# Four edits to a transformer-layer kernel: how tiles are cut into transfers, how many buffers they have, and where the softmax sums are applied

## The reference, cut to what matters

```python
# x: (2, 8192, 1024) fp32; 16 heads of 64, 4 KV heads; 8 experts, 2 picked, and a shared MLP
xn = layernorm(x)
q, k, v = xn @ Wq, xn @ Wk, xn @ Wv          # rotary embedding on q and k
attn = softmax(q @ k.T / 8 + slope[h] * (j - i))    # ALiBi bias, no causal mask
a = (attn @ v) @ Wo
scores = softmax(xn @ gate_w.T); w_dense = the two largest of 8, others 0
h = xn @ W1[e].T; y, g = split(h)            # H = 768
z = sum_e w_dense[:, e] * ((y * silu(g)) @ W2[e].T) + shared_mlp(xn)
return x + a + z
```

## Time and profile before

| | us |
|---|---|
| two runs | 4456.20 and 4581.11 |
| their median | 4518.65 |
| the profiled execution, whole | 4454.75 |
| its span, slowest core (core 4) | 4453.2 |
| spans of all eight cores | 4438.6 to 4453.2 |

### The profile page before, as it was taken

One profiled execution on the slowest core, in us unless ns is written; L12 is line 12 of the kernel. 1 busy time (PEld: TensorE's weight loads), 2 busy tenths in 40 slices (PEclk: granted clock), 3 DMA queues, 4 the chain that ended last, 5 costly groups with the idle time before them and its releaser, 6 DMA issues. The chain is left out here.

```text
span 4453.2 us, 37344 instructions; the slowest of 8 cores (4438.6 to 4453.2 us)
## 1 busy us (share of the span) xinstructions
PE 3047.1 (68%) x12380; PEld 1144.5 (26%) x12536; DVE 1251.3 (28%) x1819; ACT 1433.3 (32%) x1561; POOL 34.4 (1%) x49
## 2 busy tenths in 40 slices
PE   2333333222778888968888988699999999999611
PEld 1111111111112222221122222244444444444311
DVE  4554554553210000022000000133233333222333
ACT  1111111110557788925578886000110001100000
POOL 0000000000000000000000000000000000000000
PEclk8656656555668999986689999899999999999855
DMA  3111111102000000000000000522102221110133
GB/s 86 50 52 48 50 52 47 38 19 38 0 0 1 1 1 1 1 38 0 1 1 1 1 1 19 104 43 40 32 15 42 43 43 29 24 34 1 36 97 93
DMA packets 112874, 136.21 MB, mean 31 GB/s; under 512 B 10408, under 2 KB 90280, under 8 KB 112688
## 3 DMA queue, kind: packets, MB, share of 16 engines
q0 software_dynamic: 22752, 52.45, 6.7%
q1 hardware_dynamic: 89936, 81.36, 6.2%
HBM read 169.43 MB, written 16.78 MB: 42 GB/s over the span
## 5 line engine op out<-in xcount | busy, mean ns | idle before, releaser
L67 ACT ACTIVATE PT_B<-PS_B,alibi_sb 128x1024 bf16<-128x1024 f32 x626 | 694.1, 1109 | 426.8 <-PE PS_B L67 426.0
L67 PE MATMUL PS_B<-Qpair,K 64*128 64x512 bf16 x1252 | 429.0, 427 | 161.2 <-ACT PT_B L67 146.6
L67 ACT ACTIVATE PT_A<-PS_A,alibi_sb 128x1024 bf16<-128x1024 f32 x428 | 476.6, 1113 | 117.1 <-PE PS_A L67 82.4
L67 PE MATMUL PVB<-PT_B,V 128*65 128x512 bf16 x1252 | 442.1, 440 | 45.1 <-DVE prewo L67 44.5
L67 PE MATMUL PA<-xn,w1sb 128*128 128x512 bf16 x1881 | 438.4, 390 | 33.8 <-DVE wbc L67 28.2
L67 PE MATMUL PB<-xn,w1sb 128*128 128x512 bf16 x1882 | 421.9, 379 | 2.0
L67 PE MATMUL TP<-id_sb,xntm 128*128 128x128 bf16 x640 | 80.9, 306 | 499.6 <-DVE xntm L67 366.1
L67 ACT ACTIVATE gact<-PA 128x1024 f32<-128x1024 f32 x60 | 61.4, 1023 | 871.4 <-PE PA L67 871.4
L67 ACT ACTIVATE lns<-vvs,eps_sb 128x1 f32<-128x1 f32 x80 | 23.5, 294 | 826.4 <-DVE vvs L67 826.4
L67 PE MATMUL PVA<-PT_A,V 128*65 128x512 bf16 x856 | 276.9, 406 | 10.1 <-ACT PT_B L67 10.0
L67 PE MATMUL PS_A<-Qpair,K 64*128 64x512 bf16 x856 | 275.5, 404 | 7.2 <-ACT PT_A L67 6.9
(11 more groups left out here) (121 smaller groups left out, 2375.2 us busy)
## 6 DMA issues: line engine op xcount, KB each, us to landing
xt<-xb SPq DMA_DIRECT2D x256, 128.0 KB, 2.4
w1sb<-w1t POOLq DMA_DIRECT2D x20, 1536.0 KB, 17.0
w2sb<-w2t POOLq DMA_DIRECT2D x20, 768.0 KB, 9.6
xt<-xown SPq DMA_DIRECT2D x64, 128.0 KB, 2.4
zacc<-zst SPq DMA_DIRECT2D x16, 512.0 KB, 2.6
zin<-zacc SPq DMA_DIRECT2D x32, 256.0 KB, 3.5
xtb<-xown SPq DMA_DIRECT2D x64, 128.0 KB, 3.5
out<-osb SPq DMA_DIRECT2D x64, 128.0 KB, 2.0
```

The lines of the kernel that those rows point to most:

```text
L67: ins = getattr(e, m)(*a, **kw)
```

## The change

It makes four edits and leaves the arithmetic as it is.

1. Stage A: `xt` has two slots instead of four, and a tile comes with one transfer of 128 x 1024 instead of four of 128 x 256. SP waits for tile `tau - 2`.
2. Stage B: `pend_evac`, `defer` and the closures are gone. At every pair's end the code records `recB`, `recA`, `nrmB`, `nrmA` in place, before the next pair.
3. Stage C: each of `w1` and `w2` comes with one transfer instead of two.
4. Stage D: `zin`, `xtb` and `out` come and go with one transfer each instead of two, four and four, and all buffers of the stage, `PO` included, have four slots instead of two. The order on SP, with its wait at line 1091, stays.

```diff
-            if tau >= 4:
-                r.wait("sync", V, v_xt_done[tau - 4])
-                r.wait("sync", S, s_xt_done[tau - 4])
-            sxp = sx[tau % 4]
-            for ch in range(4):
-                r.op("sync", "dma_start", xt[:, tbx + ch * 256: tbx + (ch + 1) * 256],
-                     src_r[:, lt, ch * 256:(ch + 1) * 256], inc=[(sxp, 16)])
+            if tau >= 2:
+                r.wait("sync", V, v_xt_done[tau - 2])
+                r.wait("sync", S, s_xt_done[tau - 2])
+            sxp = sx[tau % 2]
+            r.op("sync", "dma_start", xt[:, tb:tb + 1024], src_r[:, lt, :], inc=[(sxp, 16)])
...
-                if it < len(pend_evac):
-                    pend_evac[it]()
...
-            if defer:
-                def chunk1():
-                    recA()
-                    nrmB()
-                pend_evac = [recB, chunk1, nrmA]
-            else:
-                recB(); recA(); nrmB(); nrmA()
-                pend_evac = []
+            r.wait("scalar", T, t_pv[len(kcs) - 1])
+            r.op("scalar", "activation", rtmp[64:65, 0:1024], PVB[64:65, :], AF.Ln)
+            r.chain("scalar")
+            r.op("scalar", "activation", rlb[64:65, 1024:2048], rtmp[64:65, 0:1024],
+                 AF.Exp, scale=-1.0, inc=[(S, 1)])
+            s_recB = S.v
...
+            for head, PVx, hh, s_rec in ((1, PVB, hB, s_recB), (0, PVA, hA, s_recA)):
+                r.wait("tensor", S, s_rec)
+                for st in range(2):
+                    r.op("tensor", "matmul", PVx[64:128, st * 512:(st + 1) * 512],
...
-        for ch in range(2):
-            r.op("gpsimd", "dma_start",
-                 w1sb[:, buf * 12288 + ch * 6144: buf * 12288 + (ch + 1) * 6144]
-                 .rearrange("p (dc f) -> p dc f", dc=4),
-                 w1_d[e].rearrange("(dc p) f -> p dc f", p=128)[:, ch * 4:(ch + 1) * 4, :],
-                 inc=[(gw[buf], 16)])
+        r.op("gpsimd", "dma_start",
+             w1sb[:, buf * 12288:(buf + 1) * 12288].rearrange("p (dc f) -> p dc f", dc=DC),
+             w1_d[e].rearrange("(dc p) f -> p dc f", p=128), inc=[(gw[buf], 16)])
...
-        bb = (tb % 2) * 1024
-        s4p = s4[tb % 2]
-        if tb >= 2:
-            r.wait("sync", V, v_used[tb - 2])
-        for ch in range(2):
-            r.op("sync", "dma_start",
-                 zin[:, bb + ch * 512: bb + (ch + 1) * 512].rearrange(
-                     "p (dc c) -> p dc c", dc=4),
-                 z_r[:, ch * 4:(ch + 1) * 4, tb * 128:(tb + 1) * 128], inc=[(s4p, 16)])
-        for ch in range(4):
-            r.op("sync", "dma_start", xtb[:, bb + ch * 256: bb + (ch + 1) * 256],
-                 xo_r[:, tb, ch * 256:(ch + 1) * 256], inc=[(s4p, 16)])
+        bb = (tb % 4) * 1024
+        s4p = s4[tb % 4]
+        if tb >= 4:
+            r.wait("sync", V, v_used[tb - 4])
+        r.op("sync", "dma_start", zin[:, bb:bb + 1024].rearrange("p (dc c) -> p dc c", dc=DC),
+             z_r[:, :, tb * 128:(tb + 1) * 128], inc=[(s4p, 16)])
+        r.op("sync", "dma_start", xtb[:, bb:bb + 1024], xo_r[:, tb, :], inc=[(s4p, 16)])
...
         r.wait("sync", V, V.v)
-        for ch in range(4):
-            r.op("sync", "dma_start", out_d[tb * 128:(tb + 1) * 128, ch * 256:(ch + 1) * 256],
-                 osb[:, bb + ch * 256: bb + (ch + 1) * 256], inc=[(so[tb % 2], 16)])
-        ds_out[tb] = so[tb % 2].v
+        r.op("sync", "dma_start", out_d[tb * 128:(tb + 1) * 128, :], osb[:, bb:bb + 1024],
+             inc=[(so[tb % 4], 16)])
+        ds_out[tb] = so[tb % 4].v
```

More of the change, by code:

```diff
@@ L178, in build_nc @@
     gset = Ctr(top, nc, "gset")
-    sx = [Ctr(top, nc, f"sx{i}") for i in range(4)]
+    sx = [Ctr(top, nc, "sx0"), Ctr(top, nc, "sx1")]
     scs = Ctr(top, nc, "scs")
@@ L183, in build_nc @@
     ga = [Ctr(top, nc, "ga0"), Ctr(top, nc, "ga1")]
-    s4 = [Ctr(top, nc, "s4a"), Ctr(top, nc, "s4b")]
-    so = [Ctr(top, nc, "so0"), Ctr(top, nc, "so1")]
+    s4 = [Ctr(top, nc, f"s4_{i}") for i in range(4)]
+    so = [Ctr(top, nc, f"so{i}") for i in range(4)]
     sdbg = Ctr(top, nc, "sdbg")
@@ L761, in build_nc @@
                 v_qpair = V.v
[L762 to L801, removed]
-                    else:
-                        v_pvA_free = V.v
-                    v_prewo_done = V.v
-                return emit
@@ new lines, in build_nc @@
+            r.op("scalar", "activation", rtmp[64:65, 0:1024], PVB[64:65, :], AF.Ln)
[3 more added lines that the diff above has]
+            s_recB = S.v
+            r.chain("scalar")
+            r.op("scalar", "activation", rtmp[64:65, 0:1024], PVA[64:65, :], AF.Ln)
+            r.chain("scalar")
+            r.op("scalar", "activation", rlb[64:65, 0:1024], rtmp[64:65, 0:1024],
+                 AF.Exp, scale=-1.0, inc=[(S, 1)])
@@ L824, in build_nc @@
+            s_recA = S.v
             if p < 7 and not do_prebuild:
                 v_qpair, v_psA_next = emit_qbuild(p + 1, gate_s=sB[63], gate_t=t_qkB)
-            t_pv_prev = t_pv_last
+            for head, PVx, hh, s_rec in ((1, PVB, hB, s_recB), (0, PVA, hA, s_recA)):
+                r.wait("tensor", S, s_rec)
+                for st in range(2):
+                    r.op("tensor", "matmul", PVx[64:128, st * 512:(st + 1) * 512],
+                         ones64[64:65, 0:64],
+                         rlb[64:65, head * 1024 + st * 512: head * 1024 + (st + 1) * 512],
+                         start=True, stop=True, skip_group_check=True)
+                r.inc_last("tensor", T)
+                t_bc = T.v
+                r.wait("vector", T, t_bc)
+                ro = (hh % 2) * 64
+                co = (hh // 2) * 1024
+                for st in range(2):
+                    r.op("vector", "tensor_copy", rb_sb[:, :],
+                         PVx[64:128, st * 512:(st + 1) * 512])
+                    r.op("vector", "tensor_mul",
+                         prewo[ro:ro + 64, co + st * 512:co + (st + 1) * 512],
+                         PVx[0:64, st * 512:(st + 1) * 512], rb_sb[:, :],
+                         inc=[(V, 1)])
+                if head == 1:
+                    v_pvB_free = V.v
+                else:
+                    v_pvA_free = V.v
@@ L827, in build_nc @@
+            v_prewo_done = V.v
+            t_pv_prev = t_pv[len(kcs) - 1]
             sA63_prev = sA[63]
@@ L1034, in build_nc @@
     d_sc = ExitStack()
-    zin = d_sc.enter_context(nc.sbuf_tensor("zin", [128, 2048], F32))
-    xtb = d_sc.enter_context(nc.sbuf_tensor("xtb", [128, 2048], F32))
-    zhi = d_sc.enter_context(nc.sbuf_tensor("zhi", [128, 2048], BF16))
-    zhi32 = d_sc.enter_context(nc.sbuf_tensor("zhi32", [128, 2048], F32))
-    zlo = d_sc.enter_context(nc.sbuf_tensor("zlo", [128, 2048], BF16))
-    osb = d_sc.enter_context(nc.sbuf_tensor("osb", [128, 2048], F32))
-    PO1 = d_sc.enter_context(nc.psum_tensor("PO1", [128, 1024], F32))
-    PO2 = d_sc.enter_context(nc.psum_tensor("PO2", [128, 1024], F32))
+    zin = d_sc.enter_context(nc.sbuf_tensor("zin", [128, 4096], F32))
+    xtb = d_sc.enter_context(nc.sbuf_tensor("xtb", [128, 4096], F32))
+    zhi = d_sc.enter_context(nc.sbuf_tensor("zhi", [128, 4096], BF16))
+    zhi32 = d_sc.enter_context(nc.sbuf_tensor("zhi32", [128, 4096], F32))
+    zlo = d_sc.enter_context(nc.sbuf_tensor("zlo", [128, 4096], BF16))
+    osb = d_sc.enter_context(nc.sbuf_tensor("osb", [128, 4096], F32))
+    POs = [d_sc.enter_context(nc.psum_tensor(f"PO{i}", [128, 1024], F32))
+           for i in range(4)]
     r = Rec(SELFS)
```

57 lines of the change are left out of this document (18 added, 39 removed).

## The result

| | before | after |
|---|---|---|
| median of all runs | 4544.62 (26) | 4449.01 (27) |
| fastest run | 4445.55 | 4400.16 |
| profiled execution, whole | 4454.75 | 4404.17 |
| spans of the eight cores | 4438.6 to 4453.2 | 4393.5 to 4402.6 |

The change makes the kernel faster by 1.2%: the ratio is 0.988, with a 95% interval of 0.9846 to 0.9913. The two medians lie further apart than that, because both kernels have executions in which some cores ran at a lower clock; the ratio leaves these out. On 4454.75 us the ratio is 53 us, with the interval 39 to 69. I had forecast 28 less, a ratio of 0.994, which lies outside. So the direction was right and the size was not.

A forecast was written before the change was run, and what follows sets the result against it. Four stages with different limits: A a chain of short steps, B PE and ACT, C PE's speed, D a serial loop. 4454.75 - 26 (D) - 2 (B) + 0 (A, C) gave 4427 us, range 4390 to 4500 for 8 in 10.

The forecast's parts named there:

- Stage D, -26: Stage D: merging ten issues a tile into three saves 1.6 us a tile, 26 us over 16 tiles.
- bounds of 1.0 and 4.2: Stage D, gain in us a tile: 1.0 if the data rate limits, 4.2 if only issues and one large landing count.
- Stage A and C, 0: Stages A and C: no gain or cost, A's transfers staying hidden and C's first weight wait ending with the same byte.
- Stage B, -2: Stage B: ten turns at +0.1 us each and two turns from pair 5 to 6 at -1.5 each, together -2 us.
- The bound of -18: Stage B's largest gain from the rows: ten turns at -0.9 us and two at -4.3.
- Rival 1: Stage D is bound by issue, not data, and gains up to 67 us: 4386 us in all; chance 0.12.
- Rival 2: Stage D: the merged transfers bring nothing, 4453 us in all; chance 0.15.
- Rival 4: Stage A loses its cover from a 9.25 us landing on; at 11 us it costs 140 us, 4567; chance 0.02.
- Rival 3: Stage B: in-place sums cost what the first chunk loses, 6.15 us a turn, 74 us: 4503 in all; chance 0.10.
- Within 2%: Whole kernel: time changes by no more than 2%, between 4366 and 4544 us; chance 0.91.
- Slower: Whole kernel: slower by over 2%, above 4544 us; chance 0.05.
- The likeliest case's own range: Whole kernel: 4405 to 4441 us, with stage D's gain between 16 and 40 and B's between -10 and +4.

The follow-up runs named there:

- d_only: The kernel before with stage D's edit alone (merged transfers, four slots); stage D 233.7 us, ratio 0.9966 [0.9916, 1.0016].
- ac_only: The kernel before with the edits of stages A and C alone; A 1070.8 us, C 1395.5 us, ratio 0.9988 [0.9954, 1.0021].
- before_fill: The kernel before, deferral kept, with throw-away matmuls in PE's wait in a pair's second chunk; stage B 1695.0 us, whole run 4427.77 us.
- b_in_place: The kernel before with stage B's edit alone, sums in place at all 12 turns; stage B 1698.8 us, ratio 0.995 [0.9923, 0.9976].
- fill_chunk: The changed kernel with one throw-away matmul in each B-only chunk after the prebuild; stage B 1679.4 us, ratio 0.9896 [0.979, 1.0003].
- d_xtb: The kernel before with only stage D's four `xtb` transfers merged into one; stage D 254.8 us, whole run 4500.40 us.

## Why the prediction was right in places and wrong in the sum

**Stage D, -26: right, with luck in the size.** Measured -27.4, and -27 alone in `d_only`. A tile takes 14.6 us where "about 14.5" was said, the stage 233 where "near 230" was said, and the four slots alone save nothing. The 1.6 us a tile, chosen between bounds of 1.0 and 4.2, was 1.5 between the cores shown. But the fastest cores in pieces take 15.6 us a tile and the merged ones 14.4 to 14.6, a gain of 1.1 us, close to the bound of 1.0 that the rate of the data gave. The rest is that the pieces landed later in this execution of before (`xtb` after a median of 3.4 to 3.8 us by core) than on those fastest cores (3.1), which no term had. Nor did the prediction say how the gain divides: most of it belongs to `out`, the transfer nobody waits for, because its issues stand ahead of the inputs'.

**Stage A and C, 0: right.** `ac_only` and the wait rows agree.

**Stage B, -2: wrong, it is -20.** Two steps failed. The first is the frame: "What counts is the time from the last exponential of a pair to the fourth of the next, after which both orders run alike." They run the same instructions after it, but not at the same speed. The deferred order leaves PE at half clock longer, in the fifth to eighth chunk and beyond. The prediction had 0 us there; the runs have -10.6, and `before_fill` shows that it is the clock.

The second is the size of the terms up to the fourth exponential, -2 forecast and -7.6 measured. The first exponential in place was right (9.1 us at nearly all turns, 9.11 from the earlier trace rows). At the ordinary turns the fourth came after 15.9 to 17.2 us, half of them above the 16.4 that was the upper bound. But the deferred order has 16.0 to 17.9 there, and the 16.04 taken for all ten turns came from a single one, 4 to 5. At the turn from 5 to 6 the fourth exponential was forecast after 19.3 us, -1.5; it came after 18.1 and 17.8 in the two halves, -2.6 and -3.0. The timeline of ACT and PE there in after, core 4, answers the earlier trace rows:

```profile
1570.86 1.11 ACT L67 ACTIVATE PT_B<-PS_B,alibi_sb 128x1024 bf16<-128x1024 f32 x1
...
1580.11 5.29 PE L67 MATMUL PS_A<-xn,wq_sb 128*128 128x512 bf16 x15 [0.33 <-issue]
...
1589.16 1.11 ACT L67 ACTIVATE PT_A<-PS_A,alibi_sb 128x1024 bf16<-128x1024 f32 x1
```

The prebuild takes 0.35 us a matmul, between the 0.23 of full clock and the 0.42 of half (5.06 / 12 in `before_fill`), and I had placed it near half; the wait of 8.22 us for `prewo` is gone.

Counted to the pairs' last exponentials, the turn from 5 to 6 is worth -4.2 and -2.6. The ten others were taken as one kind at +0.1. The turn from 4 to 5 is indeed at -0.05 and -0.6, but the one from 0 to 1 is at -3.7 and -3.5. Its lateness stood in the trace of before, with the fourth exponential at 17.9 us instead of 16.0. The other six turns and those from 4 to 5 together give -4.3. So the terms are 2 x -3.4 and 10 x -1.15 instead of 2 x -1.5 and 10 x +0.1.

The bound of -18 that the rows gave for B lies close to the truth by luck: it holds gains up to the fourth exponential alone, of which 7.6 us came.

**The rivals.** Rival 1, D bound by issue, did not come (233 us, not 191). Rival 2, nothing from merging, is refuted by `d_only` (233.7 us in D, where kernels with all pieces have 253.7 to 275.9), and the rule of the Trainium skill behind it doesn't hold here either. Rival 4, stage A without cover, did not come: one wait of 0.3 us. Rival 3, the sums in place cost what the first chunk loses, has the mechanism right and the sign wrong. I wrote that "a turn that leaves PE at half clock adds 0.43 us to each B-only chunk that ran at full clock", and counted it against the order with the sums in place. It counts against the deferred order: its waits for `PVB`, 2.99 and 8.22 us, come in the middle of the chunks.

The Trainium skill's "TensorE: Matmul & The Clock Gate" (Why this matters for your kernels) asks for no longer idle gaps between bursts of matmuls. The runs agree with that (1716 to 1695 us from keeping PE busy), and the mistake was to apply it to one of two orders when both have gaps.

**Range and chances.** The median of after, 4449.01, lies in 4390 to 4500; that says little, since the base moved as well. "Within 2%" holds for the ratio of 0.988. "Slower" had no ground. The likeliest case's own range should have ended at 4443 us (4454.75 - 16 + 4), not 4441; nothing hangs on it.

## What to carry to other kernels

When work is moved about on an engine that waits, compare not only when the next step begins but at which clock the engine comes out of it, and read every turn rather than one: here the order with the later start was the faster, and a dozen throw-away matmuls in a wait gave as much as the reordering. Compare cores and executions that are alike before a small difference is divided among causes. More buffers do nothing until the loads are issued ahead of the wait that blocks the queue; with loads two tiles in advance, the kernel won another 100 us in the stage where the merging had won 18 to 27. On a queue that feeds a serial loop, first cut the issues that stand ahead of the inputs.

## What the runs showed that I had not expected

- The clock's half level outlives a short wait: after waits of 2.40 and 1.22 us PE ran some 10 us at half clock (to 1434.2 in the turn shown), and one added matmul per chunk in the stretches that the earlier trace rows has at 0.50 shortened stage B by 17 us.
- Stage C took 1450 to 1454 us instead of 1396 on two neighbouring cores, in three of the runs (cores 6 and 7 of `b_in_place`, 2 and 3 of `fill_chunk`, 4 and 5 of `d_xtb`), with no edit there in common. The granted clock of the stage was 0.92 on these cores and 0.96 on the others. It was neither of the two levels for 300 to 333 us of the stage, but 0.81, as in this window of `d_xtb`, core 4, while core 6 had 0.99:

```profile
4046.00:4195.00 149.00, 144.58 (x551) 59.57 (x550) 32.03 (x27) 12.28 (x12) 0.00 (x0) 0.81 0.00 0
```

- The same stands behind a stage B of 1743 to 1747 us instead of 1716 on cores 6 and 7 of `d_xtb` (0.82 instead of 0.86 over the stage) and one of 1712 and 1713 instead of 1696 on cores 4 and 5 of `b_in_place`. What lowers the clock of two cores and not of the others stays open.
- In pieces, stage D varied by 35 us between pairs of cores over the runs (250 to 285), merged by 4.
